# Cross attention and output stage in one program, the output weights split during the last groups, splits of the next batch's context on POOL

## The chip, the cores and the metric

One core of a Trainium2 chip runs the kernel. The metric is device time in microseconds of one execution; a row of runs is given by its median. The engines are TensorE (PE, and PEld for its weight loads), VectorE (DVE), ScalarE (ACT), GpSimd (POOL) and SyncE (SP), which issues all DMAs. Each engine works through its own instructions in order and waits on semaphores.

## The reference

A decoder block on x (4 batches of 256 rows, 512 wide) with a context of 1601 rows per batch, all in float32:

```python
x = _layernorm(x + _L0_attn_ref(x, w_qkv, w_o))                      # 32 heads of 128, 8 kv heads, causal, rotary
x = _layernorm(x + _L0_xattn_ref(x, ctx_4096, Wq, Wk, Wv, Wo))       # 16 heads of 96, 4 kv heads
x = _layernorm(x + _L0_ffn_ref(x, lora_A, lora_B, W, bias, lora_w))  # x @ W.T + bias + low-rank adapters
```

The cross attention takes its keys and values from the context and the latents together (1601 + 256 rows, padded to 1858):

```python
hidden = jnp.concatenate([context, latents], axis=1)
q, k, v = latents @ Wq.T, hidden @ Wk.T, hidden @ Wv.T
attn = softmax(q @ k / sqrt(96))
out = (attn @ v) @ Wo.T
```

## The kernel before

Three programs follow each other: `self_attention`, `cross_attention` and `finish`. Each has a block of its own, and a program begins only when all engines have ended the one before. All of TensorE's large products are taken with float32 operands split in two parts, a high part (a copy to the type float32r, made by ACT) and a low part (the difference from the original, made by DVE or POOL), and three products: high by high, high by low, low by high (`PARTS`).

`cross_attention` goes over the 4 batches. For each it projects keys and values from the context in seven chunks (`projection_steps`), whose splits are the steps "hidden": ACT copies the chunk of 128x1024 (L1004), POOL subtracts in four pieces of 128x256 (L1287). Then come 8 groups (4 kv heads by 2 halves of the queries) of 8 steps (`PAIRS`), 64 steps in a batch (`attention_steps`). A step k is for TensorE six matmuls of scores (L1132) and six of values for step k - 2 (L1145), and, except in the last group, two matmuls (L1103) for the row maxima of the next group. The eighth step of a group is half as long. ACT takes the exponential (L1202) into b_pf and copies its high part to b_pr (L989), DVE makes the low part (L995, both inputs in SBUF) and reduces the maxima (L1251). At j = 3 DVE works out the reciprocals of the row sums (L1263 to L1267), at j = 4 ACT spreads them (L1217) and POOL multiplies (L1294), whose result y SP stores to the tensor "attended". Queries are loaded into b_qraw per kv head and split in the steps "queries": ACT's copy L1174, POOL's subtraction L1298, both 96x1024, at j = 6 of groups 2 and 4. In groups 3 and 5 at j = 6 the first two context chunks of the next batch are split.

One schedule, `schedule_b`, lists the steps of all batches. Each engine runs through this list and does its own part of each step, in the list's order; what holds it is only the semaphores in its part. So an engine without a part in a step goes past it.

SP issues loads and stores in an order of its own (L1026 to L1062). In the last batch it loads for the output stage, as soon as the projections are done: the attended rows of batch 0 (`y_first`), the output weights (`wo_raw`), the feed weights (`wt`) and the adapters.

`finish` first splits the 12 pieces of the output weights and of batch 0's attended rows (ACT L1440 and L1437, DVE L1461, POOL L1510). Its TensorE part, for eight tiles of 128 rows, is `project(t)` (36 matmuls of 512 columns; ahead of the last nine stands `turn(t - 1)`, four transposes of the normed tile), then `feed(t - 1)` (12 matmuls with the feed weights). After the first tile stand the `adapters` (four float32 matmuls, whose results DVE adds to `wt`). DVE and ACT take the norms in the order of the list `norms`, each (t, 0) after the output product and (t, 1) after the feed; a norm is an add, statistics, a root on ACT (L1447), a reciprocal and a scaling (L1504). DVE makes the turned tile's low part (L1472) at the beginning of norm (t + 1, 0), for the last tile at the beginning of (7, 1). ACT copies its high part (L1455) behind the root of (t, 0).

## Time and profile before

| | us |
|---|---|
| median of 3 runs | 1933.54 (1930.08 to 1937.99) |
| the profiled execution | 1935.04 |
| its span, first to last instruction | 1933.2 |
| self attention and its hand-over | 0 to about 750 |
| four batches of cross attention | about 750 to 1815 |
| output stage | about 1817 to 1933 |

In rows of a timeline the columns are the start in us from the span's beginning, the duration in us, the engine, the line, the operation, output and inputs, the count, and in brackets the idle time before it with what ended it. A row can stand for several instructions in a run (xN), and its duration then reaches from the first to the last.

### The profile page before, as it was taken

Reading aid. Unit: us, or ns where it says so; the run is one execution under the profiler, and the core shown is the slowest. Engines: PE = TensorE matmul, PEld = TensorE weight load, DVE = VectorE, ACT = ScalarE, POOL = GpSimd, SP = SyncE. Lnnn points to the kernel's source line nnn. Section 1 sums busy time; section 2 is a strip of 40 time slices with the busy share of each in tenths; the row PEclk is TensorE's granted clock in tenths of the full one; section 3 lists DMA queues with packets and bytes.
Section 4 is the critical chain, followed back from the end, with each engine's and each line's share of the span. In section 5 each row is a group of like instructions: output and inputs, shape, how many; then the busy total and the mean of one; then the engine's idle time right before and its main releaser. Section 6 shows DMA issues by size and latency. Waiting matters only on the chain. (4 is left out here: it accounts for less than half of the span.)

```text
span 1933.2 us, 28030 instructions
## 1 busy us (share of the span) xinstructions
PE 1874.4 (97%) x9512; PEld 1542.0 (80%) x9512; DVE 1229.7 (64%) x2123; ACT 1184.8 (61%) x2081; POOL 654.3 (34%) x682
## 2 busy tenths in 40 slices
PE   7999999999999999999999999999999999999798
PEld 5888888888888788877779877788777798777576
DVE  4665656566566712577865678745778656787654
ACT  5666656666566633467775577764677755777620
POOL 5666757667576522101103011121011030110341
PEclk8999999999999999999999999999999999999899
DMA  4001101001010354100102000111001023000220
GB/s 170 28 28 28 48 11 49 27 27 43 11 54 13 114 193 126 55 5 17 28 20 79 11 9 27 28 39 55 5 17 28 20 77 133 9 17 9 90 82 27
DMA packets 59384, 89.84 MB, mean 46 GB/s; under 512 B 7060, under 2 KB 42260, under 8 KB 58518
## 3 DMA queue, kind: packets, MB, share of 16 engines
q1 hardware_dynamic: 59288, 88.57, 14.5%
...
## 5 line engine op out<-in xcount | busy, mean ns | idle before, releaser
L1145 PE MATMUL b_o_ps<-b_pr,b_v 128*97 128x512 f32 (+1 forms) x1440 | 376.2, 395 | 12.0 <-DVE b_pr L995 10.7
L1132 PE MATMUL b_s<-b_q,b_kt 97*128 97x512 f32 (+1 forms) x1440 | 374.8, 394 | 2.0 <-DVE b_v L1244 2.0
L1251 DVE TENSOR_REDUCE b_mx<-b_m 128x1 f32<-128x1024 f32 (+1 forms) x256 | 286.7, 1120 | 120.6 <-PE b_m L1103 119.3
L995 DVE TENSOR_TENSOR b_pr<-b_pf,b_pr 128x1024 fp32r<-128x1024 f32 (+1 forms) x256 | 310.1, 1211 | 67.6 <-ACT b_pr L989 67.6
L1202 ACT ACTIVATE b_pf<-b_s 128x1024 f32<-128x1024 f32 (+1 forms) x256 | 247.5, 967 | 135.8 <-PE b_s L1132 135.3
L1145 PEld LDWEIGHTS b_o_ps<-b_pr,b_v 128*97 128x97 f32 (+1 forms) x1440 | 231.8, 162 | 111.8 <-ACT b_pr L989 12.1
L1132 PEld LDWEIGHTS b_s<-b_q,b_kt 97*128 97x128 f32 (+1 forms) x1440 | 262.7, 185 | 64.6 <-issue 3.7
L1294 POOL TENSOR_TENSOR b_y<-b_recs,b_o 96x512 f32<-96x512 f32 x32 | 41.3, 1290 | 768.7 <-ACT b_recs L1217 768.7
L989 ACT ACTIVATE b_pr<-b_pf 128x1024 fp32r<-128x1024 f32 (+1 forms) x256 | 257.5, 1006 | 42.0 <-PE b_o_ps L1145 38.5
L445 PE MATMUL a_ring<-a_xt,w_a 128*128 128x512 f32 x1128 | 278.9, 398 | 0.0
L445 PEld LDWEIGHTS a_ring<-a_xt,w_a 128*128 128x128 f32 x1128 | 208.8, 191 | 41.0
L495 PE MATMUL a_ring<-a_wo,a_y 128*128 128x512 f32 x768 | 191.2, 398 | 0.0
L800 POOL TENSOR_TENSOR a_p<-a_p,a_rec 128x128 f32<-128x128 f32 (+1 forms) x256 | 130.5, 530 | 143.3 <-DVE a_rec L704 143.3
L495 PEld LDWEIGHTS a_ring<-a_wo,a_y 128*128 128x128 f32 x768 | 140.2, 189 | 29.2 <-DVE a_y L714 1.0
L1103 PE MATMUL b_m<-b_kt,b_q 96*128 96x512 f32 (+1 forms) x512 | 152.5, 379 | 1.8 <-DVE b_mx L1251 1.8
L1083 PE MATMUL b_s<-a_hid,w_kv 128*128 128x256 f32 (+1 forms) x1008 | 130.0, 286 | 6.8 <-issue 4.9
L1083 PEld LDWEIGHTS b_s<-a_hid,w_kv 128*128 128x128 f32 x1008 | 127.8, 189 | 9.4 <-issue 5.7
L605 ACT ACTIVATE a_p<-a_ms,a_top 128x128 f32<-128x128 f32 (+1 forms) x256 | 114.2, 448 | 31.0 <-DVE a_top L698 29.4
L1087 PE MATMUL b_s<-w_kv,a_hid 128*128 128x384 f32 (+1 forms) x720 | 133.0, 337 | 0.0
L698 DVE CUSTOM_DVE_ANT_0 a_ms<-a_s,a_mask 128x128 f32<-128x128 f32 (+1 forms) x256 | 81.1, 354 | 80.3 <-PE a_s L462 80.0
L1287 POOL TENSOR_TENSOR a_hid<-hraw,a_hid 128x256 fp32r<-128x256 f32 (+1 forms) x108 | 75.7, 732 | 165.0 <-ACT a_hid L1004 165.0
L1087 PEld LDWEIGHTS b_s<-w_kv,a_hid 128*128 128x128 f32 (+1 forms) x720 | 123.6, 184 | 3.3
...
## 6 DMA issues: line engine op xcount, KB each, us to landing
...
```

The lines of the kernel that those rows point to most:

```text
L445: mm = pe.matmul(bank[:], w[:, a, c, t * HD:(t + 1) * HD], xt[:, m, c, n * HALF:(n + 1) * HALF], start=i == 0, stop=i == 3 * C - 1)
L495: mm = pe.matmul(bank[:], y[:, b % 2, a, h, tt * P:(tt + 1) * P], wo[:, m, h, :], start=i == 0, stop=i == 3 * GRP - 1)
L800: pool.tensor_tensor(seen, seen, rec[:, h, qt:qt + 1].to_broadcast([P, (qt + 1) * P]), ALU.mult)\
L989: act.activation(pr[0:rows, k % 2, HI, 0:n], pf[0:rows, k % 2, 0:n], ACT.Copy).then_inc(p_hi.sem, 1)
L995: dve.tensor_tensor(pr[0:rows, k % 2, LO, 0:n], pf[0:rows, k % 2, 0:n], f(pr[0:rows, k % 2, HI, 0:n]), ALU.subtract).then_inc(p_lo.sem, 1)
L1083: mm = pe.matmul(bank[:, 0:n], w_k[:, a, c, i * P:(i + 1) * P], hid[:, j % 2, m, c, 0:n], start=s == 0, stop=s == 3 * C - 1)
L1087: mm = pe.matmul(bank[0:rows, 0:KV2 * HD2], hid[:, j % 2, a, c, t0 - c0:t0 - c0 + rows], w_v[:, m, c, :], start=s == 0, stop=s == 3 * C - 1)
L1103: mm = pe.matmul(ps_m[:, x:min(x + BANK, n)], q[0:HD2, kv % 2, HI, hp * BANK + t * P:hp * BANK + (t + 1) * P], kt[0:HD2, HI, kv, c0 + x:c0 ...
L1132: mm = pe.matmul(ps_s[k % 2][0:rows, i * BANK:(i + 1) * BANK], kt[:, a, kv, t0:t0 + rows], q[:, kv % 2, m, hp * BANK:(hp + 1) * BANK], sta ...
L1145: mm = pe.matmul(ps_o[0:HD2 + 1, :], v[0:rows, a, t, g // 2, :], pr[0:rows, k % 2, m, i * BANK:(i + 1) * BANK], start=t == 0 and s == 0, s ...
L1202: act.activation(pf[0:rows, k % 2, 0:n], ps_s[k % 2][0:rows, 0:n], ACT.Exp, scale=SCALE_B)\
L1251: dve.reduce_max(mx[:, g % 2, t, half:half + 1], ps_m[:, 0:MAXW[half][1]], X).then_inc(mx_made.sem, 1)
```

## The change

- `finish` is gone. Its tiles lie over SBUF and PSUM that the cross attention no longer needs in its last batch, so that it all is one block. For this b_v and b_kt are laid out by kv head first, and the kv heads' values stand in rotated order (`slot`, and the host's order of `wv`).
- In the last batch the 12 pieces of the output weights and batch 0's attended rows are split in steps "wo2", one in each step from group 6, j = 2 on: ACT copies the weights' piece (128x512); POOL copies and subtracts the rows' piece (128x256) and subtracts the weights' piece. DVE's scaling of the adapters' operand is a step at group 7, j = 2.
- The first tile of the output product (`output(0)`) stands ahead of the last two value steps and of the sums of the last group. The adapters follow, and their sums by DVE.
- The query splits for kv = 2 and 3 are done by POOL alone (a copy and a subtraction), listed at j = 1 instead of 6 of groups 2 and 4. The next batch's context splits in groups 3 and 5 are also done by POOL alone.
- The turned tile and the feed's PSUM have two buffers, x2 three. The order at the end changes: `output(7)` directly behind `output(6)`, then the feeds of tiles 5 and 6, the last transposes and the last feed; norm (5, 1) stands behind (7, 0).
- The loads of x1, of the bias and of batch 1's attended rows are issued earlier, in the last groups.

The core of the diff:

```diff
-def attention_steps():
+def attention_steps(last):
 
     s = []
+    work = [("wo2", k) for k in range(FT)]
...
-        if g in (2, 4) and j == 6:
-            s += [("queries", g // 2 + 1)]
+        if g in (2, 4) and j == 1:
+            s += [("queries", g // 2 + 1, "spare")]
         if g in (3, 5) and j == 6:
-            s += [("hidden", g // 2 - 1, "next")]
+            s += [("hidden", g // 2 - 1, "spare", "next")]
+        if last and work and (g == GROUPS - 2 and j >= 2 or g == GROUPS - 1):
+            s += [work.pop(0)]
+        if last and (g, j) == (GROUPS - 1, 2):
+            s += [("lora",)]
     return s + [("split", STEPS - 1)]
 
 
...
-    body = attention_steps()
     tail = [("pv", STEPS - 2), ("pv", STEPS - 1), ("sums", GROUPS - 1), ("spread", GROUPS - 1)]
     s = []
     for b in range(B):
         head = projection_steps(b > 0)
+        body = attention_steps(b + 1 == B)
         s += [(x, b) for x in (head if b == 0 else head[FRONT:])]
         if b + 1 == B:
-            s += [(x, b) for x in body + tail if x[-1] != "next"]
+            s += [(x, b) for x in body + [("first_rows",)] + tail if x[-1] != "next"]
             break
         s += [(x[:-1], b + 1) if x[-1] == "next" else (x, b) for x in body]
...
-        kt = sb("b_kt", [ROWB + 1, 2, KV2, S2], F32R)
-        v = sb("b_v", [P, 2, NT2, KV2, HD2 + 1], F32R)
+        v_mem = nc.sbuf_base
+        v = sb("b_v", [P, KV2, 2, NT2, HD2 + 1], F32R)
+        kt_mem = nc.sbuf_base
+        kt = sb("b_kt", [ROWB + 1, KV2, 2, S2], F32R)
+        q_mem = nc.sbuf_base
...
+        wo_s = over(early_mem, "c_wo", [P, 2, FT, D], F32R)
+        y0_mem = early_mem + 4 * 2 * FT * D
+        y_in0 = over(y0_mem, "c_y0", [P, 2, FT, T], F32R)
+        x2t_mem = y0_mem + 4 * 2 * FT * T
+        assert x2t_mem + 4 * 2 * D <= kt_mem + 3 * 4 * 2 * S2
+        x2t = [over(x2t_mem, "c_x2t0", [P, 2, D], F32R), over(v_mem, "c_x2t1", [P, 2, D], F32R)]
+        x2 = over(v_mem + 4 * 2 * D, "c_x2", [P, 3, D])
+        assert 4 * 5 * D <= v_head
+        y_in1 = over(w_mem, "c_y1", [P, 2, FT, T], F32R)
+        y_c = (y_in0, y_in1)
...
+        ps_w = [ps_s[0][:, i * BANK:(i + 1) * BANK] for i in range(2)]
+        ps_f = [ps_s[1][:, i * BANK:(i + 1) * BANK] for i in range(2)]
+        ps_y = [ps_m[:, i * BANK:(i + 1) * BANK] for i in range(2)]
...
+        norms = []
+        for t in range(TILES + 1):
+            norms += [(t, 0)] * (t < TILES) + [(t - 1, 1)] * (1 <= t < TILES - 1)
+        norms += [(TILES - 2, 1), (TILES - 1, 1)]
+        norms.remove((TILES - 3, 1))
+        norms.insert(norms.index((TILES - 1, 0)) + 1, (TILES - 3, 1))
+        nth = {x: i for i, x in enumerate(norms)}
...
+        def spare(arg):
+
+            return arg[-1] == "spare"
...
                 for g in range(GROUPS):
+                    if b == END and g == GROUPS - 1:
+
+                        sp.wait_ge(s_made.sem, s_made.at(b, STEPS))
+                        sp.dma_start(x1[:, 0:2, :], x1_dram[:, 0:2, :]).then_inc(x1_in[0], 16)
+                        load_attended(1)
+                        sp.dma_start(x1[:, 2:TILES, :], x1_dram[:, 2:TILES, :]).then_inc(x1_in[1], 16)
...
+                    if g == 4:
+                        sp.wait_ge(q_lo.sem, q_lo.at(b, KV2))
+                        if b + 1 < B:
+                            load_queries(b + 1, 0)
+                        else:
+                            sp.dma_start(bias_s[:], bias.to_broadcast([P, D])).then_inc(bias_in, 16)
...
+            for b in range(2, B):
+                sp.wait_ge(y_lo, FT * b)
+                load_attended(b)
...
+
+            def output(t):
+                b = t // 2
+                if t >= 2:
+                    pe.wait_ge(z_done, nth[(t - 2, 0)] + 1)
+                else:
+                    pe.wait_ge(mx_made.sem, mx_made.at(END, 8 * GROUPS))
+                for k in range(FT):
+                    if k == FT - 3 and t:
+                        turn(t - 1)
+                    if t % 2 == 0:
+                        pe.wait_ge(y_lo, FT * b + k + 1)
+                    if t == 0:
+                        pe.wait_ge(wo_lo, k + 1)
+                    for i, (a, m) in enumerate(PARTS):
+                        mm = pe.matmul(ps_y[t % 2], y_c[b % 2][:, a, k, (t % 2) * P:(t % 2 + 1) * P], wo_s[:, m, k, :],
+                                       start=k == 0 and i == 0, stop=k == FT - 1 and i == 2)
+                mm.then_inc(y_full, 1)
+
+            def turn(t):
+                pe.wait_ge(normed, nth[(t, 0)] + 1)
+                if t:
+                    pe.wait_ge(t_lo, t)
+                for c in range(C):
+                    mm = pe.transpose(ps_t[:, c * P:(c + 1) * P], x2[:, t % 3, c * P:(c + 1) * P], idf[:])
+                mm.then_inc(turned, 1)
+
+            def feed(t):
+                pe.wait_ge(t_hi, t + 1)
+                pe.wait_ge(t_lo, t + 1)
+                pe.wait_ge(w_lo, C)
+                if t >= 2:
+                    pe.wait_ge(z_done, nth[(t - 2, 1)] + 1)
+                i = 0
+                for c in range(C):
+                    for a, m in PARTS:
+                        mm = pe.matmul(ps_f[t % 2], x2t[t % 2][:, a, c * P:(c + 1) * P], ws[:, m, c, :], start=i == 0,
+                                       stop=i == 3 * C - 1)
+                        i += 1
+                mm.then_inc(f_full, 1)
+
+            def adapters():
+
+                pe.wait_ge(lb_done, 1)
+                pe.wait_ge(exp_done.sem, exp_done.at(END, STEPS))
+                for c in range(C):
+                    if c >= 2:
+                        pe.wait_ge(w_sum, c - 1)
+                    pe.matmul(ps_w[c % 2], la[:, c * P:(c + 1) * P], lb[:], start=True, stop=True).then_inc(w_full, 1)
 
...
+                elif kind == "first_rows":
+                    output(0)
 
             run(pe, handle)
+            adapters()
+            for t in range(1, TILES):
+                output(t)
+                if t < TILES - 2:
+                    feed(t - 1)
+            feed(TILES - 3)
+            feed(TILES - 2)
+            turn(TILES - 1)
+            feed(TILES - 1)
...
-                if kind == "hidden":
+                if kind == "hidden" and not spare(arg):
                     split_hidden(act, b, arg[0])
-                elif kind == "queries":
+                elif kind == "queries" and not spare(arg):
...
+                elif kind == "wo2":
+                    k = arg[0]
+                    if k == 0:
+                        act.wait_ge(late_in.sem, 16 * len(last_loads))
+
+                        act.wait_ge(pv_done.sem, pv_done.at(b, (GROUPS - 2) * PAIRS))
+                    act.activation(wo_s[:, HI, k, :], woraw[:, k, :], ACT.Copy).then_inc(wo_hi, 1)
...
+            act.wait_ge(pv_done.sem, pv_done.at(END, STEPS))
+            for c in range(C):
+                act.wait_ge(w_sum, c + 1)
+                act.activation(ws[:, HI, c, :], wt[:, c, :], ACT.Copy).then_inc(w_hi, 1)
+            for i, (t, which) in enumerate(norms):
+                act.wait_ge(eps_done, i + 1)
+                act.activation(std[:, i % 2:i % 2 + 1], mv[:, i % 2, 1:2], ACT.Sqrt).then_inc(std_done, 1)
+                if which == 0:
+                    if t % 2 == 0 and t // 2 + 1 < B:
+                        for k in range(0, FT, 4):
+                            split_y(t // 2 + 1, k, 4)
+                    act.wait_ge(turned, t + 1)
+                    if t >= 2:
+                        act.wait_ge(f_full, t - 1)
+                    act.activation(x2t[t % 2][:, HI, :], ps_t[:], ACT.Copy).then_inc(t_hi, 1)
...
+                elif kind == "lora":
+                    dve.wait_ge(late_in.sem, 16 * len(last_loads))
+                    dve.wait_ge(lw_in, 16)
+                    dve.tensor_scalar(lb, lb, lw[:, 0:1], ALPHA_OVER_RANK, ALU.mult, ALU.mult).then_inc(lb_done, 1)
...
+            dve.wait_ge(pv_done.sem, pv_done.at(END, STEPS))
             for c in range(C):
                 dve.wait_ge(w_full, c + 1)
-                dve.tensor_tensor(wt[:, c, :], ps_w[c % 2][:], wt[:, c, :], ALU.add).then_inc(w_sum, 1)
...
+                    if spare(arg):
+                        pool.wait_ge(h_in.sem, h_in.at(b, 16 * C * (j + 1)))
+
+                        pool.wait_ge(full.sem, full.at(b, 0))
+                        pool.tensor_copy(hid[:, j % 2, HI, :, 0:n], hraw[:, :, 0:n]).then_inc(h_hi.sem, 1)
...
+                elif kind == "wo2":
+                    k = arg[0]
+                    if k == 0:
+                        pool.wait_ge(late_in.sem, 16 * len(last_loads))
+                        pool.wait_ge(pv_done.sem, pv_done.at(b, (GROUPS - 2) * PAIRS))
+                    pool.tensor_copy(y_in0[:, HI, k, :], y_first[:, k, :]).then_inc(y_hi, 1)
+                    pool.wait_ge(y_hi, k + 1)
+                    pool.tensor_tensor(y_in0[:, LO, k, :], y_first[:, k, :], f(y_in0[:, HI, k, :]), ALU.subtract).then_inc(y_lo, 1)
+                    pool.wait_ge(wo_hi, k + 1)
+                    pool.tensor_tensor(wo_s[:, LO, k, :], woraw[:, k, :], f(wo_s[:, HI, k, :]), ALU.subtract).then_inc(wo_lo, 1)
...
+                    if spare(arg):
+                        pool.wait_ge(q_in.sem, q_in.at(b, 16 * (kv + 1)))
+
+                        pool.wait_ge(s_made.sem, s_made.at(b, (kv - 1) * 2 * PAIRS))
+                        pool.tensor_copy(q[0:HD2, kv % 2, HI, :], qraw[:]).then_inc(q_hi.sem, 1)
+                    pool.wait_ge(q_hi.sem, q_hi.at(b, kv + 1))
+                    pool.tensor_tensor(q[0:HD2, kv % 2, LO, :], qraw[:], f(q[0:HD2, kv % 2, HI, :]), ALU.subtract)\
```

## Rows read from the trace of the kernel before

**Rows 1.** The page: busy TensorE, clock granted in 40 slices, costliest group.
```profile
PE 1874.4 (97%) x9512; PEld 1542.0 (80%) x9512; DVE 1229.7 (64%) x2123; ACT 1184.8 (61%) x2081; POOL 654.3 (34%) x682
...
PEclk8999999999999999999999999999999999999899
...
L1145 PE MATMUL b_o_ps<-b_pr,b_v 128*97 128x512 f32 (+1 forms) x1440 | 376.2, 395 | 12.0 <-DVE b_pr L995 10.7
```

**Rows 2.** Timeline of POOL, y products of groups 3 and 4, later 2 to 4.
```profile
1171.49 1.28 POOL L1294 TENSOR_TENSOR b_y<-b_recs,b_o 96x512 f32<-96x512 f32 x1 [17.84 <-ACT b_recs L1217]
...
1196.34 1.29 POOL L1294 TENSOR_TENSOR b_y<-b_recs,b_o 96x512 f32<-96x512 f32 x1 [15.45 <-ACT b_recs L1217]
...
1678.88 1.28 POOL L1294 TENSOR_TENSOR b_y<-b_recs,b_o 96x512 f32<-96x512 f32 x1 [23.30 <-ACT b_recs L1217]
...
1704.74 1.30 POOL L1294 TENSOR_TENSOR b_y<-b_recs,b_o 96x512 f32<-96x512 f32 x1 [17.84 <-ACT b_recs L1217]
1729.19 1.29 POOL L1294 TENSOR_TENSOR b_y<-b_recs,b_o 96x512 f32<-96x512 f32 x1 [23.15 <-ACT b_recs L1217]
```

**Rows 3.** Timeline of the last batch, end of group 4, with a query split.
```profile
1733.66 1.04 ACT L1174 ACTIVATE b_q<-b_qraw 96x1024 fp32r<-96x1024 f32 x1
...
1734.79 2.40 POOL L1298 TENSOR_TENSOR b_q<-b_qraw,b_q 96x1024 fp32r<-96x1024 f32 x1 [4.30 <-ACT b_q L1174]
...
1735.69 2.58 DVE L995 TENSOR_TENSOR b_pr<-b_pf,b_pr 128x1024 fp32r<-128x1024 f32 x1
...
1738.42 1.59 PE L1145 MATMUL b_o_ps<-b_pr,b_v 128*97 128x512 f32 x6 [1.12 <-DVE b_pr L995]
```

**Rows 4.** Timeline of the last batch, end of group 5, without a split.
```profile
1760.13 0.85 PE L1132 MATMUL b_s<-b_q,b_kt 97*65 97x512 f32 x3
...
1761.47 1.22 DVE L995 TENSOR_TENSOR b_pr<-b_pf,b_pr 128x1024 fp32r<-128x1024 f32 x1
...
1762.95 1.57 PE L1145 MATMUL b_o_ps<-b_pr,b_v 128*97 128x512 f32 x6
```

**Rows 5.** Groups of POOL by form, whole span: busy us, mean ns, idle before.
```profile
L1287 POOL TENSOR_TENSOR a_hid<-hraw,a_hid 128x256 fp32r<-128x256 f32 x92 | 71.0, 803 | 136.5 <-ACT a_hid L1004 136.5
...
L1517 POOL TENSOR_TENSOR c_ws<-wt,c_ws 128x512 fp32r<-128x512 f32 x4 | 5.0, 1297 | 4.0 <-ACT c_ws L1444 4.0
```

**Rows 6.** Timeline of the hand-over from the attention to the output stage.
```profile
1807.38 1.56 PE L1145 MATMUL b_o_ps<-b_pr,b_v 128*97 128x512 f32 x6
...
1809.40 2.29 PE L1145 MATMUL b_o_ps<-b_pr,b_v 128*97 128x512 f32 x9 [0.46 <-DVE b_pr L995]
...
1813.37 0.70 DVE L1267 STREAM_TRANSPOSE b_recs<-b_rec 32x512 f32<-32x512 f32 x1
...
1817.51 0.63 ACT L1440 ACTIVATE c_wo<-wo_raw 128x512 fp32r<-128x512 f32 x1 [2.14 <-PEq L907]
...
1819.51 5.90 PE L1387 MATMUL c_y<-c_wo,c_y 128*128 128x512 f32 x15 [7.81 <-POOL c_y L1510]
...
1833.25 3.79 PE L1418 MATMUL c_w<-lora 128*128 128x512 f32 x8
...
1836.48 6.70 PE L1387 MATMUL c_y<-c_wo,c_y 128*128 128x512 f32 x27
```

**Rows 7.** Timeline of the tail, from the last tile's last nine output matmuls.
```profile
1914.07 2.31 PE L1387 MATMUL c_y<-c_wo,c_y 128*128 128x512 f32 x9
...
1916.52 3.06 PE L1408 MATMUL c_f_ps<-c_ws,c_x2t 128*128 128x512 f32 x12
...
1919.17 0.69 DVE L1488 TENSOR_TENSOR c_x<-c_x,c_bias 128x512 f32<-128x512 f32 x1
...
1919.41 0.60 PE L1396 MATMUL c_t_ps<-idf,c_x 128*128 128x128 f32 x4
...
1922.71 0.68 DVE L1472 TENSOR_TENSOR c_x2t<-c_t_ps,c_x2t 128x512 fp32r<-128x512 f32 x1
...
1923.49 4.38 PE L1408 MATMUL c_f_ps<-c_ws,c_x2t 128*128 128x512 f32 x12 [3.48 <-DVE c_x2t L1472]
```

289 lines of the change are left out of this document (91 added, 198 removed).

## The prediction

> **What bounds the kernel now.** I read the page's busy rows first, then its costliest groups with what ended their idle time, then the timeline where the diff touches. TensorE is busy for 97% of the span; the clock granted to it dips only at the start, at the change of stages and at the end [rows 1]. So a microsecond is won only where TensorE is idle or slowed by a feeder, and three such places lie in the diff: the waits for b_pr in the attention, 10.7 us in all [rows 1], the hand-over to the output stage (an idle time of 7.81, and a slow first tile) [rows 6], and the last feed (3.48) [rows 7]. The profiled run took 1935.04 us, 1.84 above its span; the median of the three runs is 1933.54, 1.5 less. I sum changes on the profiled span and take them from the median.
>
> **What the ACT splits cost in the attention.** The y products (L1294) stand once in each group, at j = 4, so their distance is a group's period. With a query split it is 1704.74 - 1678.88 = 25.86 us, without any split 24.45, with a context split 1196.34 - 1171.49 = 24.85 [rows 2]. The other groups repeat this within 0.15. So a query split costs some 1.3 us (two in each of four batches: 10.6) and a context split 0.35 (two in each of three batches: 2.1): 12.7 us at most.
>
> Why a query split costs that stands in one group end [rows 3]. ACT's copy of 1.04 us delays b_pr's high part. Then DVE's low part (L995) takes 2.58 us instead of 1.22 [rows 4]: POOL's L1298 runs from 1734.79 to 1737.19 and L995 ends 1.08 after that, so it waited for POOL's instruction and then ran. TensorE idles 1.12 us. This is a rule of the Trainium skill, page "SBUF — State Buffer", section "Who interferes with whom": a VectorE instruction with two SBUF inputs and a GpSimd instruction that reads SBUF exclude each other for a whole instruction. By that rule work moved to POOL is not free, and the trace agrees (2.58 against 1.22 us).
>
> **Query splits on POOL.** The step stands at j = 1, but POOL knows only its own order: behind the y product of the group before, it waits for q_in and for the last scores of the old keys. So it starts right behind the last scores of the group before. For kv = 2 the load has landed long before. At such a group end [rows 4] the last scores end at 1760.98, L995 starts at 1761.47 and ends at 1762.69, and the matmul that needs it starts at 1762.95: a slack of about 0.1 us beside 0.15 of signalling. POOL's copy would start 0.1 behind the scores, 0.4 ahead of L995. With a copy of C us, L995 ends at 1761.1 + C + 1.08, and TensorE waits C - 0.65. No row shows a POOL copy. The nearest is the subtraction of the same 96x1024 tile from two inputs, 2.40 us [rows 3], my upper bound; half of it, 1.2, is the lower one, as a copy reads half as much. I take 1.5, nearer to the half because the second input is the main difference. Wait 0.85 instead of 1.3: 0.45 won four times, 1.8 us (bounds -1.8 and +3.0). The Trainium skill, page "GPSIMD Engine Reference", section "Performance versus the Vector engine", has 769 ns for a tight loop over 512 elements of one input, which would be an estimate of 1.54 us for 1024; no row can show it. The subtraction behind the copy meets only the low part of the short last step, whose matmul stands behind twelve matmuls of scores; nothing is lost there.
> For kv = 3 the load is issued behind the y product of j = 4 and lands 4 to 6 us later, when L995 has begun; in three batches POOL also has the context split ahead of it. L995 then mostly goes first. I take 1.0 of 1.3 won, four times: 4.0 us (bounds 1.5 and 5.2).
> **Context splits on POOL.** POOL starts them, too, right behind the y product. ACT's share of the 0.35 goes. But the four subtractions, 0.80 us each in the mean [rows 5], then reach over the group end with its slack of 0.1, and each can hold L995. I take 0.1 won six times: 0.6 us (bounds -1.5 and +2.1). The transfers that wait for these parts are issued a group later, so none comes late.
> Sum in the attention: 1.8 + 4.0 + 0.6 = 6.4 us won (bounds -1.8 and +10.3).
>
> **Output weights split in groups 6 and 7.** Before, the twelve pieces were split in the open: the first output matmul is at 1819.51, the adapters only at 1833.25 [rows 6]. Now ACT has one copy more per step, 0.63 us [rows 6], where it idles 0.4 to 0.7 us ahead of its high parts and exponentials, so the high part comes about 0.1 later, and up to 0.7 right behind the spread copies. POOL has per step a copy of 128x256 (0.3 to 0.6), a subtraction of that size (0.7) and one of 128x512 (1.30) [rows 5]: 2.3 to 2.6. With the 1.08 of L995, which excludes them [rows 3], that is 3.4 to 3.7 us for a step of 24.45 / 8 = 3.06 [rows 2]. L995 waits for the rest of POOL's current instruction, 0.45 in the mean and 1.3 at worst, with a slack of 0.5 to 1.4 inside a group. I take 1.5 us lost (bounds 0 and 5); DVE's one scaling of the adapters' operand, new in group 7, is in that bound.
> POOL itself comes late, but for whom? It can start behind pv(47), at about 1768.5. Twelve pieces of 2.5 and two y products of 1.3 are 32.6 us. Until 1807.5, the last scores, there are 39, less 15 low parts of 1.08, plus 2 in which waits of both overlap: 25. So the last piece is ready at 1807.5 + 7.6 = 1815.1. TensorE reaches it behind pv(61) and eleven pieces: 1807.4 + 1.4 + 11 x 0.69 = 1816.4. I take 0.5 us lost (bounds 0 and 4). Group 6's y product stands behind ten pieces on POOL, at about 1809. For it wait the copy of o of group 7 (due at 1819) and, on SP, its store and the loads of x1 and of the next attended rows behind that.
>
> **The hand-over.** Before: from pv(61) at 1807.38 to the second tile at 1836.48, 29.1 us [rows 6]. After, in TensorE's order and at 1.39 us for six matmuls of 512 columns (half of the 2.78 that a feed adds): pv(61) 1.39, the 36 matmuls of the first tile 8.33, the 9 of pv(62) and pv(63) 2.08, sum 11.8. Then four adapters of (1836.48 - 1833.25) / 4 = 0.81 each. Two run at once; the third waits for DVE's first sum, now behind the sums of group 7. These reached before from 1811.69 to 1814.07 [rows 6], 2.4 us; with 0.7 for the sum and 0.15 of signalling it is 3.3, of which two adapters cover 1.6. So 5.0 us instead of 3.2, in all 16.8: 12.3 less (bounds 11 and 13). The half-speed matmuls behind the idle 7.81 are in the 29.1 already. The first norm and its table load are hidden by 27 matmuls (6.3 us) ahead of the first transposes, against about 5 us of DVE and ACT. The loads of x1 and of the next attended rows, issued near 1810 now, land in 4 to 13 us; the first rows of x1 are due at 1825, the attended rows at 1828.
>
> **The tail.** The pace of a tile stays, since the low part of the turned tile sets each feed as before. At the end feed(5) goes behind output(7), and DVE has norm (7,0), then (5,1), (6,1), and only then the last turned tile's low part. Before, feed(7) starts 7.1 us after the end of output(7) at 1916.38 [rows 7]. After, counted from that end: (7,0) is done at 2.9. (5,1) needs a root from ACT, but ACT first waits for the last transposes, which stand behind two feeds (2 x 2.89, 0.1, 0.6: 6.5), and copies for 0.6, so (5,1) ends near 8.0. (6,1) takes 3.5 (1919.17 to 1922.71), the low part 0.7 [rows 7]: feed(7) starts at 12.3. Output(7) ends 2.9 earlier, since feed(5) is not ahead of it. 12.3 - 2.9 - 7.1 = 2.3 us later. TensorE idles 5.7 us ahead of it instead of 3.48, and its 12 matmuls took 4.38 there against 3.06 before the pause [rows 7]: 0 to 0.8 more, I take 0.4. Tail: 2.7 us lost (bounds 2 and 3.5).
>
> **Sum.** 1933.54 - 12.3 - 6.4 + 1.5 + 0.5 + 2.7 = 1919.5, given as 1920 us. The new layouts of kt and v alter neither instructions nor sizes. This case alone lies within 1914 to 1925.
>
> **Rivals.**
> *POOL's copy is as slow as its subtraction.* C = 2.4: the kv = 2 splits lose 1.8 instead of winning 1.8, the context splits lose 1, each piece costs POOL 0.3 more and the first tile waits 4 us. 3.6 + 1.6 + 3.5 = 8.7 more: 1928 us. The change would then not do what it says, as POOL has no spare time that counts. For it: all of POOL's rows have nearly one rate per element [rows 3, 5]. Against: all have two inputs.
> *All of the splits' cost is won.* 12.7 instead of 6.4, and the pieces cost nothing: 1912 us. For it: POOL's long idle times [rows 2]. Against: the slack of 0.1 [rows 4].
> *The new order hides the tail.* If the last low part waited for no norm, feed(7) would start at 8.0 - 2.9, 2.0 earlier than before: 1920 - 4.7 = 1915 us. Against: DVE's program order.
> *POOL's pieces starve L995: slower than before.* If POOL is never idle in the last two groups, every L995 may meet a fresh 1.30 us subtraction, and a low part held like that cost 1.1 us [rows 3]. 14 steps x 1.1 = 15.4, and 4 us of backlog in the first tile: 19.4 in place of 2.0 gives 1937 us, and beyond 1943 if the copies are slow as well. It decides from the point where POOL's instructions and L995 exceed a step's 3.06 us, which they do by 0.3 to 0.6. Against it: L995 meets the start of the long one only now and then.
>
> **Chances.** Forecast 0.50, slow copy 0.20, all won 0.15, tail hidden 0.10, L995 starved 0.05. The range reaches over the slow copy and the full gain: 1911 to 1929. A measurement can tell about 0.5%, 9.7 us, from no change, so faster means below 1923.9. Faster: 0.43 of the forecast, 0.15, 0.10: 0.68. Same: 0.07 + 0.20 + 0.02 = 0.29. Slower 0.03.
>
> **What would show it.** The first output matmul right behind pv(61); 5 us for the adapters with a wait of 1.7; POOL's copy ahead of an L995 of 2 us and more at the end of group 1; L995 at 1.2 to 2.5 in groups 6 and 7; group periods of 24.5 to 25.4 in place of 25.86; an idle time of 5 to 6 us ahead of the last feed. I am wrong if no L995 waits for the copy, if the first tile waits for pieces for over 4 us, or if the last feed follows output(7) in less than 11 us.

## The result and the profile after

| | before | after |
|---|---|---|
| median, us | 1935.73 (11 runs, 1930.08 to 1937.99) | 1925.87 (11 runs, 1923.79 to 1931.16) |
| the profiled execution, its span | 1935.04, 1933.2 | 1924.93, 1923.0 |
| ratio after / before | | 0.9956, interval 0.9946 to 0.9966 |

The change wins 0.4%: 8.5 us of 1935 by the ratio (6.6 to 10.5), 10.2 by the two profiled spans. Expected were 14. (The median of before is here that of 11 runs, 2.2 us above the median of three that the prediction subtracts from.) The page of after, its busy rows, the granted clock in 40 slices and the first group of TensorE:

```profile
PE 1870.8 (97%) x9512; PEld 1541.8 (80%) x9512; DVE 1231.2 (64%) x2111; ACT 1168.6 (61%) x2055; POOL 708.7 (37%) x720
...
PEclk8999999999999999999999999999999999999999
...
L1234 PE MATMUL b_o_ps<-b_pr,b_v 128*97 128x512 f32 (+1 forms) x1440 | 375.9, 394 | 5.5 <-DVE b_pr L1061 4.9
```

The waits for b_pr fell from 10.7 us [rows 1] to 4.9, and in this row the granted clock no longer dips at the change of stages. In finer windows it still does, only later: it is 1.00 from 1800 to 1822 us, then 0.76 from 1822 to 1828.2, where TensorE stands idle, and 0.56 from 1828.2 to 1832.5. L1234, L1061 and L1253 of after are L1145, L995 and L1387 of before.

**Attention.** (pv(k) stands for the value matmuls of step k, output(t) for the output product of tile t, counted from 0.) The timeline of after at the end of a group with a query split for kv = 2 (POOL, DVE, TensorE), then y products of POOL:

```profile
859.34 1.03 POOL L1539 CAST b_q<-b_qraw 96x1024 fp32r<-96x1024 f32 x1 [4.80 <-PE b_s L1221]
859.69 1.76 DVE L1061 TENSOR_TENSOR b_pr<-b_pf,b_pr 128x1024 fp32r<-128x1024 f32 x1
860.46 3.26 POOL L1541 TENSOR_TENSOR b_q<-b_qraw,b_q 96x1024 fp32r<-96x1024 f32 x1
861.60 1.61 PE L1234 MATMUL b_o_ps<-b_pr,b_v 128*97 128x512 f32 x6 [0.25 <-DVE b_pr L1061]
...
853.25 1.29 POOL L1532 TENSOR_TENSOR b_y<-b_recs,b_o 96x512 f32<-96x512 f32 x1 [59.88 <-ACT b_recs L1370]
...
878.23 1.29 POOL L1532 TENSOR_TENSOR b_y<-b_recs,b_o 96x512 f32<-96x512 f32 x1 [14.51 <-ACT b_recs L1370]
902.78 1.29 POOL L1532 TENSOR_TENSOR b_y<-b_recs,b_o 96x512 f32<-96x512 f32 x1 [23.27 <-ACT b_recs L1370]
...
927.76 1.29 POOL L1532 TENSOR_TENSOR b_y<-b_recs,b_o 96x512 f32<-96x512 f32 x1 [13.38 <-ACT b_recs L1370]
```

POOL's copy takes 1.03 us, not 1.5. DVE's low part starts 0.35 behind the copy's start, waits for its end and then runs (1.76 in place of 1.22 [rows 4]); POOL's subtraction, next in line, is held by it in turn (3.26 for 2.40). The first period (853.25 to 878.23) has the kv = 2 copy in it and is 24.98. The second, which held a query split before and took 25.86 [rows 2], is 24.55. The third has the context split and behind it the kv = 3 split, and is 24.98; with the context split alone it took 24.85 before [rows 2]. The periods of the other batches repeat these within 0.03; in the last one, without a context split, the third is 25.09. So 0.4 is still lost to each kv = 2 copy and to each context split, and 0.5 to the kv = 3 split of the last batch, where no context split stands ahead of it.

**Groups 6 and 7 and the hand-over.** The longest of two waits for b_pr in groups 6 and 7, then TensorE over the hand-over (last scores' values, first tile, adapters three and four, second tile):

```profile
1783.00 1.30 POOL L1526 TENSOR_TENSOR c_wo<-wo_raw,c_wo 128x512 fp32r<-128x512 f32 x1
1783.47 1.92 DVE L1061 TENSOR_TENSOR b_pr<-b_pf,b_pr 128x1024 fp32r<-128x1024 f32 x1 [3.44 <-ACT b_pr L1055]
1785.49 1.60 PE L1234 MATMUL b_o_ps<-b_pr,b_v 128*97 128x512 f32 x6 [1.10 <-DVE b_pr L1061]
...
1799.03 1.60 PE L1234 MATMUL b_o_ps<-b_pr,b_v 128*97 128x512 f32 x6
...
1800.47 8.34 PE L1253 MATMUL b_m<-c_wo,c_y 128*128 128x512 f32 x36
...
1813.90 1.98 PE L1286 MATMUL b_s<-lora 128*128 128x512 f32 x4 [1.29 <-DVE wt L1456]
...
1815.32 6.71 PE L1253 MATMUL b_m<-c_wo,c_y 128*128 128x512 f32 x27
```

The first tile runs its 36 matmuls without a pause in 8.34 us, and from pv(61) to the second tile it is 16.3 us; before it was 29.1 [rows 6].

**The new pause.** Between the second tile and the first turned tile (timeline of POOL, DVE and TensorE):

```profile
1815.88 5.05 POOL L1548 TENSOR_TENSOR c_ws<-wt,c_ws 128x512 fp32r<-128x512 f32 x4
...
1818.83 0.17 DVE L1491 RECIPROCAL c_rstd<-c_std 128x1 f32<-128x1 f32 x1 [0.48 <-ACT c_std L1389]
1819.03 9.17 DVE L1493 TENSOR_SCALAR c_x<-c_x,c_mv,c_rstd 128x512 f32<-128x512 f32 x1
1820.90 7.01 POOL L1552 TENSOR_TENSOR c_y<-c_yraw,c_y 128x1024 fp32r<-128x1024 f32 x3
1828.25 1.12 PE L1262 MATMUL b_x<-idf,c_x 128*128 128x128 f32 x4 [6.23 <-DVE c_x L1493]
```

The norm is ready to scale at 1819.03, well ahead of the transposes' due time of 1822.0 (1815.32 + 6.71). But the scaling, 0.55 us elsewhere, takes 9.17. POOL makes the low parts of the feed weights (four) and of batch 1's attended rows (three) in one row without a gap, and the scaling ends at 1828.20, 0.29 behind POOL's last. TensorE idles 6.23 us; the transposes (1.12 for 0.60) and the nine matmuls behind them (3.69 for 2.33) run slowly for a while: the granted clock is 0.56 there, so mostly at its lower level, 1.2 GHz, and 1.00 from 1832.5 on. From the start of output(1) to that of output(2) it was 11.85 us before and is 19.99 after: 8.1 us.

**The tail.** DVE from the scaling of norm (6,1), then the last feed and the last scaling:

```profile
1911.12 0.55 DVE L1493 TENSOR_SCALAR c_z<-c_z,c_mv,c_rstd 128x512 f32<-128x512 f32 x1
1911.59 0.68 DVE L1461 TENSOR_TENSOR c_x2t<-b_x,c_x2t 128x512 fp32r<-128x512 f32 x1
...
1912.37 5.28 PE L1274 MATMUL b_s<-c_ws,c_x2t 128*128 128x512 f32 x12 [5.74 <-issue]
...
1919.98 0.55 DVE L1493 TENSOR_SCALAR c_z<-c_z,c_mv,c_rstd 128x512 f32<-128x512 f32 x1
```

TensorE's idle time of 5.74 us ends with the last low part (L1461), made from 1911.59 to 1912.27. Output(7) ends near 1900.5; the last feed starts 11.9 later, behind the low part that stands behind norms (5,1) and (6,1), and takes 5.28 us in place of 4.38 [rows 7].

The difference of the spans, piece by piece: start of the attention -1.9 (the self attention's code is the same; this start lay anywhere from 742 to 747 in the kernels run here), attention -7.7, pieces in groups 6 and 7 +1.4 (27.79 to 29.23 from the y product made in group 6 to pv(61)), hand-over -12.8, the new pause +8.1, start of the last feed +1.9, its slower matmuls +0.9. The sum is -10.1 of -10.2.

### The profile page after: what moved, and what is told of

It reads as the page before. It is cut to its first block, busy times and chain, and to the rows that moved or that the text cites. A ratio compares the mean times of both kernels' runs of the same rounds, so it can differ in the third digit from the quotient of the medians.

```text
span 1923.0 us, 28030 instructions
## 1 busy us (share of the span) xinstructions
PE 1870.8 (97%) x9512; PEld 1541.8 (80%) x9512; DVE 1231.2 (64%) x2111; ACT 1168.6 (61%) x2055; POOL 708.7 (37%) x720
## 4 chain that ended last, share of the span: by engine, by line
PE 55%; DVE 4%; issue 1%; ACT 1%; POOLq 0%; ACTq 0%
PE b_o_ps L1234 16%; PE b_s L1221 16%; PE b_s L1172 7%; PE b_s L1176 6%; PE b_m L1192 5%; PE b_m L1253 3%; DVE b_pr L1061 1%; PE b_s L1274 1%; DVE b_mx L1428 1%; DVE c_x L1493 0%; PE b_x L1262 0%; ACT b_pf L1348 0%; DVE b_kt L1417 0%; ACT b_pr L1055 0%; PE b_x L1203 0%
## 5 line engine op out<-in xcount | busy, mean ns | idle before, releaser
L1234 PE MATMUL b_o_ps<-b_pr,b_v 128*97 128x512 f32 (+1 forms) x1440 | 375.9, 394 | 5.5 <-DVE b_pr L1061 4.9
L1061 DVE TENSOR_TENSOR b_pr<-b_pf,b_pr 128x1024 fp32r<-128x1024 f32 (+1 forms) x256 | 317.1, 1239 | 66.5 <-ACT b_pr L1055 66.5
L1234 PEld LDWEIGHTS b_o_ps<-b_pr,b_v 128*97 128x97 f32 (+1 forms) x1440 | 231.8, 162 | 104.7 <-issue 13.2
L772 POOL TENSOR_TENSOR a_swapped<-a_swapped,a_sin 128x512 f32<-128x512 f32 x80 | 106.5, 1332 | 54.5 <-ACT a_swapped L585 54.5
```

The source lines that it names most:

```text
L1061: dve.tensor_tensor(pr[0:rows, k % 2, LO, 0:n], pf[0:rows, k % 2, 0:n], f(pr[0:rows, k % 2, HI, 0:n]), ALU.subtract).then_inc(p_lo.sem, 1)
L1234: mm = pe.matmul(ps_o[0:HD2 + 1, :], v[0:rows, slot(g // 2), a, t, :], pr[0:rows, k % 2, m, i * BANK:(i + 1) * BANK], start=t == 0 and s = ...
```

## The experiments

All are edits of the changed kernel; lines are those of their own text. Where only one run was made, the trace is the result, and its time stands beside it. The theory (A where the expectations use letters): the missing gain is this one scaling, held by POOL's row of subtractions.

**POOL holds back (e1_pool_holds).**

```diff
+                if b == 1:
+                    pool.wait_ge(normed, 1)
                 for k in range(0, FT, 4):
```

> The changed kernel, but POOL waits for the first norm (normed of tile 0) before it subtracts batch 1's attended rows. Theory A (POOL's back-to-back instructions starve DVE's scaling L1493, which took 9.17 us): L1493 of tile 0 ends within 2.5 us of its start (behind what is left of the four feed-weight subtractions), TensorE's wait of 6.2 us ahead of the first transposes is gone, and with the clock kept the run is 7 to 8 us shorter than the changed kernel, near 1918. Rival B (the norm is late for another reason, as x1 arriving late or ACT's table load): the wait stays at about 6 us and the time stays near 1926.

Measured: 1918.56 us (1918.41 to 1921.19), ratio to before 0.992 (0.9903 to 0.9936), so 7.3 below the changed kernel by medians. From the second tile's start to the end it is 99.5 us by the traces, in place of 107.7, so 8.2 less; but its groups 6 and 7 took 2.2 us more than those of after, for a reason that no edit touches (see the half pieces below). Its timeline at the same place:

```profile
1817.80 5.06 POOL L1548 TENSOR_TENSOR c_ws<-wt,c_ws 128x512 fp32r<-128x512 f32 x4
1820.95 2.19 DVE L1493 TENSOR_SCALAR c_x<-c_x,c_mv,c_rstd 128x512 f32<-128x512 f32 x1
1823.28 7.19 POOL L1554 TENSOR_TENSOR c_y<-c_yraw,c_y 128x1024 fp32r<-128x1024 f32 x3 [0.42 <-DVE c_x L1493]
```

With nothing behind the four feed-weight parts the scaling ends 0.28 behind them and TensorE doesn't wait. That the pause is caused by POOL, and its price, are shown. Even here the scaling, at hand from 1820.95, was passed over at the boundary of POOL's third and fourth instruction, near 1821.6.

**Small pieces (e2_small_pieces).** Batch 1's three subtractions in twelve of 128x256.

```diff
-                    pool.tensor_tensor(y_c[b % 2][:, LO, k:k + 4, :], y_later[:, k:k + 4, :],
-                                       f(y_c[b % 2][:, HI, k:k + 4, :]), ALU.subtract).then_inc(y_lo, 4)
+                    n = 1 if b == 1 else 4
+                    for i in range(k, k + 4, n):
+                        pool.tensor_tensor(y_c[b % 2][:, LO, i:i + n, :], y_later[:, i:i + n, :],
+                                           f(y_c[b % 2][:, HI, i:i + n, :]), ALU.subtract).then_inc(y_lo, n)
```

> The changed kernel, but batch 1's attended rows are subtracted in twelve pieces of 128x256 instead of three of 128x1024, back to back. Theory A1 (DVE's two-port scaling gets no turn as long as POOL's next instruction is there): L1493 still takes 8 to 10 us. Theory A2 (it waits for the one instruction in progress, as L1061 does): L1493 takes under 2 us, and TensorE's wait ahead of the first transposes is gone.

Measured: 1926.10 us in one run.

```profile
1818.35 10.40 DVE L1493 TENSOR_SCALAR c_x<-c_x,c_mv,c_rstd 128x512 f32<-128x512 f32 x1
1820.22 8.24 POOL L1554 TENSOR_TENSOR c_y<-c_yraw,c_y 128x256 fp32r<-128x256 f32 x12
```

From 1818.35 on POOL passes thirteen boundaries, those between the pieces 0.7 us apart, and the scaling gets none of them. So it isn't the length of POOL's instructions. What is left is that the next one follows without a gap, which e11 tests.

**Another form of the scaling (e3_one_port, e9_two_inputs).** In e3 the first scaling is one of 511 columns and one of a single column; in e9 it is two instructions with two inputs each in SBUF, beside the small pieces.

```diff
+                if (t, which) == (0, 0):
+                    dve.tensor_scalar(row[:, 0:D - 1], row[:, 0:D - 1], mv[:, s, 0:1], rstd[:, s:s + 1], ALU.subtract, ALU.mult)
+                    row = row[:, D - 1:D]
```

```diff
+                if (t, which) == (0, 0):
+                    dve.tensor_tensor(row, row, mv[:, s, 0:1].to_broadcast([P, D]), ALU.subtract).then_inc(shifted, 1)
+                    dve.wait_ge(shifted, 1)
+                    dve.tensor_tensor(row, row, rstd[:, s:s + 1].to_broadcast([P, D]), ALU.mult).then_inc(normed, 1)
+                    continue
```

> The changed kernel, but the scaling of tile 0's norm is cut into 511 columns and 1 column, so that its width is odd and its rate per column should fall from the 0.55 us per 512 seen in the quiet tail to about 0.65. If the long wait belongs to the double-rate form of this one-input instruction, the two together take under 1.2 us beside POOL's subtractions and TensorE's wait is gone (7 to 8 us shorter). If any DVE instruction is held by POOL's row of subtractions, it stays at 6 us.

> As e2_small_pieces (POOL's twelve pieces of 128x256 back to back), but the scaling of tile 0's norm is done by two instructions with two SBUF inputs each (the row and the mean or the root spread over it), like the low parts that waited for one POOL instruction only. If such instructions get a turn between two of POOL's, each waits 1.3 us at most, both together take under 4 us, and TensorE's wait ahead of the first transposes (7.5 us in e2_small_pieces) is gone. If POOL's row of instructions starves every DVE instruction that shares its port, they end only behind it, some 10 us later.

Measured: 1923.77 and 1925.72 us, one run each. DVE's first instruction in e3, then in e9:

```profile
1818.12 9.17 DVE L1494 TENSOR_SCALAR c_x<-c_x,c_mv,c_rstd 128x511 f32<-128x511 f32 x1
```

```profile
1816.27 10.66 DVE L1495 TENSOR_TENSOR c_x<-c_x,c_mv 128x512 f32<-128x512 f32 x1
```

e3 decides nothing: an odd width was to give the scaling another form, but 511 columns still end 0.28 us behind POOL, as 512 did, so the run doesn't show that it did. e9 shows that an instruction with two inputs is passed over as well, so the form of the scaling isn't the cause.

**A gap between POOL's instructions (e11_drain).** Same work, same order; POOL waits for its own instruction before it issues the next.

```diff
+                if c:
+                    pool.wait_ge(w_lo, c)
                 pool.tensor_tensor(ws[:, LO, c, :], wt[:, c, :], f(ws[:, HI, c, :]), ALU.subtract).then_inc(w_lo, 1)
...
+                    if b == 1:
+                        pool.wait_ge(w_lo, C)
+                        pool.wait_ge(y_lo, FT * b + k)
```

> The changed kernel in which POOL, in its row of seven subtractions behind the adapters, waits for its own instruction before it issues the next (the four of the feed weights and the three of batch 1's attended rows). The work and its order are the same; only a short pause comes between two instructions. If DVE's first scaling (9.17 us in the changed kernel) goes without its turn because POOL's next instruction is already issued when the running one ends, the pause lets it in at the next end: 0.6 to 3.5 us, the idle time ahead of the first turned tile shrinks from 6.2 to under 1.5, and the one run is about 1919. If a pause of that size doesn't matter (POOL stays ahead of DVE at each new start), the scaling still ends just behind POOL's last subtraction, 8 to 11 us long, with a time of 1925 to 1929.

Measured: 1918.13 us in one run.

```profile
1817.70 5.61 POOL L1550 TENSOR_TENSOR c_ws<-wt,c_ws 128x512 fp32r<-128x512 f32 x4
...
1820.85 1.30 DVE L1493 TENSOR_SCALAR c_x<-c_x,c_mv,c_rstd 128x512 f32<-128x512 f32 x1
```

The four take 5.61 instead of 5.05 us, so their starts lie 0.19 further apart. (One of them lasts 1.29, so 0.15 us lies between the end of one record and the start of the next; without the wait the records meet.) The scaling now ends at 1822.15, behind POOL's third instruction, and no idle time stands ahead of the transposes. From the second tile's start to the end it is 99.1 us in place of 107.7: the whole 8.1 and some 0.5 of slow matmuls in the tail. So this small gap was enough for a scaling that was already waiting. The next scaling, at 1828.71 (2.77 us), still lost one turn: it began in a gap, but had to wait for a POOL instruction whose start is recorded 0.05 behind its own.

**The old order of the tail, and the low part earlier (e4_old_tail, e5_early_split).** e4 puts the feeds and norms back in the order of before; e5 in addition makes the last turned tile's low part ahead of norm (6,1).

```diff
-            norms += [(t, 0)] * (t < TILES) + [(t - 1, 1)] * (1 <= t < TILES - 1)
-        norms += [(TILES - 2, 1), (TILES - 1, 1)]
-        norms.remove((TILES - 3, 1))
-        norms.insert(norms.index((TILES - 1, 0)) + 1, (TILES - 3, 1))
+            norms += [(t, 0)] * (t < TILES) + [(t - 1, 1)] * (t >= 1)
...
-                if t < TILES - 2:
-                    feed(t - 1)
-            feed(TILES - 3)
-            feed(TILES - 2)
+                feed(t - 1)
```

```diff
-                    if t == TILES - 1:
-                        split_turned(t)
+                    if t == TILES - 2:
+                        split_turned(t + 1)
```

> The changed kernel with the order of feeds and norms at the end as before the change (feed(t-1) behind each output(t), norm (5,1) ahead of (7,0)). By the prediction's account of the tail: output(7) ends 2.9 us later, the last feed starts 7.1 us after it instead of 11.9 and takes 4.4 us instead of 5.3, so the run is 2.8 to 3.3 us shorter than the changed kernel. Rival (the new order hides the tail): it is 2 us longer.

> The order at the end as before the change (as in e4_old_tail), and DVE's low part of the last turned tile ahead of norm (6,1) instead of behind it. If the last feed hangs on DVE's order alone, it starts about 5.1 us after output(7)'s end (7.15 in e4_old_tail, 11.9 in the changed kernel) and, with a shorter pause, takes 3.5 to 4.4 us: 2 to 3 us shorter than e4_old_tail, 4 to 5 us shorter than the changed kernel, near 1921. If the norms set the end (DVE's chain (6,1), (7,1) runs on either way), the last feed is early but the end moves by under 1 us against e4_old_tail.

Measured: e4 1925.44 us (1924.26 to 1928.65), ratio 0.9957 (0.9943 to 0.9972); e5 1922.80 (1919.78 to 1926.97), ratio 0.9945 (0.9928 to 0.9961). The last feed of e4, then of e5 with the last scaling:

```profile
1913.31 4.57 PE L1271 MATMUL b_s<-c_ws,c_x2t 128*128 128x512 f32 x12 [3.53 <-issue]
```

```profile
1914.29 3.04 PE L1271 MATMUL b_s<-c_ws,c_x2t 128*128 128x512 f32 x12 [1.46 <-ACT c_x2t L1391]
...
1920.70 0.55 DVE L1487 TENSOR_SCALAR c_z<-c_z,c_mv,c_rstd 128x512 f32<-128x512 f32 x1
```

In e4 output(6)'s start lies 37.9 us before the end, in the changed kernel 40.1: the new order costs 2.2 us by the traces. The medians differ by only 0.4 and the spans by 0.2 the other way. The traces show why: from the y product made in group 6 to the second tile e4 took 47.7 us and after 45.5, and these 2.2 undo the 2.2 of the tail. So the cost of the order is shown by the traces alone. In e5 the last feed starts 5.05 us behind output(7) and runs at its full pace, 3.04. The end is then set by DVE: the norms (6,1) and (7,1) follow each other without a pause, and the last scaling ends 12.0 us behind output(7). The rival by which the last low part would wait for no norm was thus real as a mechanism, but it isn't what the change does.

**ACT splits again (e6_act_splits).** The query and context splits go back to ACT, the query splits also to j = 6 (ACT again waits for the last scores of the old keys).

```diff
-        if g in (2, 4) and j == 1:
-            s += [("queries", g // 2 + 1, "spare")]
+        if g in (2, 4) and j == 6:
+            s += [("queries", g // 2 + 1)]
         if g in (3, 5) and j == 6:
-            s += [("hidden", g // 2 - 1, "spare", "next")]
+            s += [("hidden", g // 2 - 1, "next")]
```

> The changed kernel with only one part undone: ACT makes the high parts of the queries (at j = 6) and of the next batch's context again. By the periods of the two traces (2.04 us won in each of the first three batches, 1.62 in the last) it is 7.7 us longer than the changed kernel, near 1933.6, with group periods of 25.8 at the query splits and L1061 (the low part) at 2.6 us there. The prediction's term was 6.4 us. If the gain of the attention is a matter of the run and not of the splits, the difference is under 3 us.

Measured: 1936.90 us (1931.91 to 1938.92), ratio 1.0012 (1.0002 to 1.0023). Two y products, a query split between them:

```profile
1193.85 1.30 POOL L1534 TENSOR_TENSOR b_y<-b_recs,b_o 96x512 f32<-96x512 f32 x1 [15.46 <-ACT b_recs L1372]
1219.69 1.30 POOL L1534 TENSOR_TENSOR b_y<-b_recs,b_o 96x512 f32<-96x512 f32 x1 [17.83 <-ACT b_recs L1372]
```

The period is 25.84 again. The profiled span is 7.1 above the changed kernel's, near the 7.7 expected from the periods; the medians say 11, and what the rest is stays open. So without the splits on POOL the change wins nothing: its hand-over gain of 12.8 is given back in the new pause (8.1), the tail (2.8) and the waits in groups 6 and 7 (1.5 in this run).

**The copy behind the low part (e7_copy_later).**

```diff
                         pool.wait_ge(s_made.sem, s_made.at(b, (kv - 1) * 2 * PAIRS))
+                        pool.wait_ge(p_lo.sem, p_lo.at(b, (kv - 1) * 2 * PAIRS - 1))
                         pool.tensor_copy(q[0:HD2, kv % 2, HI, :], qraw[:]).then_inc(q_hi.sem, 1)
```

> The changed kernel, but POOL waits, ahead of its query copy, for the low part of step 6 of the group that is ending. If the 0.4 us that a group with the kv = 2 split still costs (24.97 against 24.56) is the low part waiting behind POOL's 1.03 us copy, the period falls to 24.6 or less and no low part there takes over 1.4 us. The subtraction (2.4 us) then reaches over the short last low part, which has time for it. If the subtraction costs it, the period stays or grows.

Measured: 1927.57 us in one run (against after its attention began 2.3 us later, its groups 6 and 7 took 2.2 more, and 36 matmuls of a projection took 1.5 more; see the half pieces and the end of this text). POOL's copy and DVE's low part, at the group end shown above for after:

```profile
861.92 1.22 DVE L1061 TENSOR_TENSOR b_pr<-b_pf,b_pr 128x1024 fp32r<-128x1024 f32 x1
863.29 1.03 POOL L1540 CAST b_q<-b_qraw 96x1024 fp32r<-96x1024 f32 x1 [6.52 <-DVE b_pr L1061]
```

The low part runs its 1.22 again and the kv = 2 period falls from 24.98 to 24.51 in all four batches; so does the kv = 3 period of the last batch, from 25.09 to 24.55. The context periods stay at 24.98. The copy ahead of the low part was the 0.4, and 2.4 us in all.

**Half pieces in groups 6 and 7 (e10_half_pieces).**

```diff
-                    pool.tensor_tensor(wo_s[:, LO, k, :], woraw[:, k, :], f(wo_s[:, HI, k, :]), ALU.subtract).then_inc(wo_lo, 1)
+                    for i in range(0, D, D // 2):
+                        s = pool.tensor_tensor(wo_s[:, LO, k, i:i + D // 2], woraw[:, k, i:i + D // 2],
+                                               f(wo_s[:, HI, k, i:i + D // 2]), ALU.subtract)
+                    s.then_inc(wo_lo, 1)
```

> The changed kernel with POOL's subtraction of each output weight piece in two halves of 128x256 instead of one of 128x512, in groups 6 and 7. If TensorE's waits there come from a low part of DVE that has to wait for the rest of POOL's running instruction, as I hold, no wait for b_pr in these groups is longer than 0.7 us (half of the long instruction's 1.3 and a little), and their sum is 0.3 to 1.0 where the changed kernel has 1.5 and most of its variants 3.3. If instead DVE needs POOL to pause, or POOL's total work counts (now slightly more, 12 extra starts of some 0.06), the sum is 1.5 to 3.5 or more and single waits still reach 1.1 to 1.5. The time moves by at most 3 us, less than one look can tell; the waits are the result.

Measured: 1926.24 us in one run. TensorE's waits for b_pr in the two groups are 0.49, 0.65 and 0.37:

```profile
1785.61 1.61 PE L1234 MATMUL b_o_ps<-b_pr,b_v 128*97 128x512 f32 x6 [0.65 <-DVE b_pr L1061]
...
1800.96 7.66 PE L1253 MATMUL b_m<-c_wo,c_y 128*128 128x512 f32 x33
...
1809.24 0.94 PE L1253 MATMUL b_m<-c_wo,c_y 128*128 128x512 f32 x3 [0.62 <-POOL c_wo L1527]
```

The longest wait is 0.65, so a low part does wait for one running POOL instruction here. But the sum, 1.51, is that of the changed kernel (0.42 + 1.10), against 3.3 in e1, e2, e3, e4, e5, e7 and e8 (e8: 1.54, 0.94, 0.40 and 0.43), whose edits don't touch these groups in the last batch. With the larger sum it is 47.7 us from the y product made in group 6 to the second tile, with the smaller one (after, e6, e9, e11) 45.5, in e10 46.3. What decides between the two patterns isn't shown. A single run can differ from another by these 2.2 us, whatever its edit does elsewhere. And POOL, with twelve more starts, now comes late: its last piece ends at 1809.09 and the first tile stands 0.62 us for it. So I was wrong to expect 0.3 to 1.0.

**All together (e8_all, e12_all_half).** e8 has the edits of e1, e5 and e7 at once, e12 those and the half pieces.

> Four edits together on the changed kernel: POOL waits for the first norm before batch 1's attended rows (as in the first experiment), the old order of the tail with the last turned tile's low part ahead of norm (6,1) (as in the fifth), and POOL's copy of the kv = 2 queries behind the low part (as in the seventh). If the three gains lie at different places and simply add, as I hold: -7.3 (hold, by medians of the first experiment) -3.1 (tail, by medians of the fifth) and -1.6 (four copies of 0.4) from 1925.9, which gives 1913.9; 1911 to 1917 is within what self attention's own start varies. The idle time ahead of the first turned tile is gone and DVE's first scaling takes under 2.5 us; the last feed starts about 5 us after the end of output(7). If a pause that is filled only moves the end to the next limit (the attended rows of batch 1, or DVE's norms), less than two thirds of it comes: 1918 or more, with a new wait ahead of output(2) or at the end.

> The edits of the combined kernel and in addition the half pieces of POOL's output weights. If both work as I hold, it is 0.5 to 3 us below the combined kernel: 1911 to 1914, with no wait for b_pr in groups 6 and 7 above 0.7. If the halves do nothing for the waits, the two are within 1 us of each other.

Measured: e8 1912.81 us (1910.29 to 1913.02), ratio 0.9882 (0.9865 to 0.9899); e12 1911.72 (1909.26 to 1914.07), ratio 0.9885 (0.9868 to 0.9902). The two can't be told apart by medians; from the y product made in group 6 to the second tile e12 takes 46.3 us and e8 47.7, so by the traces the half pieces save 1.4 against this pattern. Both beat both kernels: by 22 to 23 us the one before, by 13 to 14 the changed one, where 12 had been expected of e8. The first turned tile and the last feed in e8:

```profile
1820.12 2.19 DVE L1487 TENSOR_SCALAR c_x<-c_x,c_mv,c_rstd 128x512 f32<-128x512 f32 x1
...
1822.95 0.60 PE L1259 MATMUL b_x<-idf,c_x 128*128 128x128 f32 x4
...
1901.66 3.04 PE L1271 MATMUL b_s<-c_ws,c_x2t 128*128 128x512 f32 x12 [1.46 <-ACT c_x2t L1391]
```

The first pause is gone, and ahead of the last feed 1.46 us are left of 5.74. From the second tile to the end it is 94.7 us (107.7 in the changed kernel, 96.7 before). The gains add, as they lie at different places of TensorE's chain.

## Why the prediction came out as it did

The sign, the size's order and the places were right; the forecast of 1920 us lay 6 below the measured median. Of these, 2.2 are the median of before, which is 1935.73 with 11 runs and was 1933.54 with three. The measured 1925.87 is 0.9 above the range given for this case alone (1914 to 1925). It lies in the full range only by the room left for the slow copy, which didn't come; that part of the hit is luck. "Faster", below 1923.9, had a chance of 0.68 and didn't come; the 0.29 for "same" did, though the interval shows a gain. None of the signs listed looked at the place where the time was lost. By its own steps, with the spans:

- **Hand-over, 12.3 forecast, 12.8 measured.** Right. The adapters take 4.6 us (1810.73 to 1815.32) with a wait of 1.29, for 5.0 and 1.7.
- **"The first norm and its table load are hidden by 27 matmuls."** This is the step that failed, at a cost of 8.1 us. The other terms came out at 16.3 us won, for 14.0; with the pause 8.2 is left, and the measured ratio says 8.5 (the spans have 1.9 more by the earlier start of the attention, which isn't the change's). So errors of the other terms hid 2.3 us of this one. The count of DVE's and ACT's time was good: the scaling was at hand 3.0 us before the transposes were due. I priced it at its busy time and never asked what POOL does meanwhile. Before, a gap of 0.27 us stood between the feed weights' parts and the attended rows' parts on POOL, and the same scaling, begun at 1840.19, took 0.88 (rows below). POOL's row then began 4.45 us ahead of the scaling and ended just before ACT's first copy of the attended rows. Now the last y product (1814.64 to 1815.91) stands right ahead of the row, which begins 3.15 us ahead of the scaling; the copy is ready when the fourth part ends, and no gap is left. e1 and e11 show it, each by taking away a different part of the cause: what follows the running instruction, and the lack of a gap.
```profile
1835.74 5.04 POOL L1517 TENSOR_TENSOR c_ws<-wt,c_ws 128x512 fp32r<-128x512 f32 x4 [3.96 <-ACT c_ws L1444]
...
1840.19 0.88 DVE L1504 TENSOR_SCALAR c_x<-c_x,c_mv,c_rstd 128x512 f32<-128x512 f32 x1
1841.05 7.12 POOL L1510 TENSOR_TENSOR c_y<-c_yraw,c_y 128x1024 fp32r<-128x1024 f32 x3 [0.27 <-ACT c_y L1437]
```

- **Attention, 6.4 forecast, 7.7 measured.** The mechanism was right: a wait of C - 0.65 with C = 1.03 is 0.38; the period was 0.4 longer than before and 0.5 longer than in e7, which took it away. The undersized terms are the copy (1.5 taken, 1.03 measured) and the kv = 3 splits (1.0 of 1.3 taken; in three batches all of it was won). The rate that the Trainium skill gives for a tight loop of one input (page "GPSIMD Engine Reference", section "Performance versus the Vector engine") led to an estimate of 1.54; the trace has 1.03, and decides. The context splits won nothing where I had 0.6: their period is 24.98, 0.1 above that of before.
- **Pieces in groups 6 and 7, 1.5 lost forecast, 1.4 measured**, though 3.3 in most other kernels with the same groups. L1061 was held for 0 to 0.7 us in after, up to 1.1 in e8. The rival in which these pieces starve the low part didn't come: here DVE got its turn at the first boundary each time.
- **First tile waits for the last piece, 0.5 forecast, none measured.** The whole attention ends 8.4 us earlier, so these times must be counted from pv(61) (1799.03 now). The last piece was ready 8.5 us behind it, at 1807.54, for 7.7 worked out; so POOL's work was counted 0.8 too low, not too high. TensorE came to that piece about 0.4 us later. It didn't wait, but by a small margin, as e10 shows with its 0.62.
- **Tail, 2.3 and 0.4 forecast, 1.9 and 0.9 measured.** The last feed 11.9 behind output(7), for 12.3; the idle time 5.74, for 5.7. The matmuls behind it were slowed more (5.28 us for 12) than I took, though 4.71 in e11.
- **A row misread.** The prediction has the clock dip "at the end [rows 1]"; the slices there show 9. A finer window does show it, 0.67 from 1923.4 to 1928 in before. No term of the sum rests on this.
- **Rivals.** The slow copy is refuted by 1.03 us. Of the splits' whole cost of 12.7 us 7.7 was won, so that rival failed too. The tail wasn't hidden.

**What stays open.** In the attention a low part of DVE that meets a row of POOL instructions got its turn at the first boundary: L1061 at 1783.47 above, and L995 in the kernel before, which took 1.62 us amid four subtractions of 128x256:

```profile
1177.08 3.81 POOL L1287 TENSOR_TENSOR a_hid<-hraw,a_hid 128x256 fp32r<-128x256 f32 x4 [4.31 <-ACT a_hid L1004]
1177.98 1.62 DVE L995 TENSOR_TENSOR b_pr<-b_pf,b_pr 128x1024 fp32r<-128x1024 f32 x1
```

In the first norm DVE's instruction got none of four boundaries (after) or thirteen (e2 and e9). Neither the length of POOL's instructions (e2), nor the number of inputs of DVE's (e9) explains the difference (neither 1024 columns nor an fp32r output was tried on DVE's side there); a scaling of DVE in group 7 (the adapters' operand, at 1787.48, 1.53 us) waited for one instruction only. Shown is that without a gap it can be passed over until POOL's row ends, and that gaps of 0.15 us ended that in e11. The Trainium skill, page "SBUF — State Buffer", section "Who interferes with whom", says: "Whoever issues first gets the shared pair for the whole instruction". The trace agrees at the group end shown first: the low part waits for the copy that began 0.35 ahead of it, and POOL's subtraction then waits for the low part. The second scaling of e11 doesn't fit, if the records' starts are taken as the order: recorded 0.05 ahead of POOL's instruction, it waited for it to end. Who is next when an instruction ends the sentence doesn't say, and by the traces here that need not be the one that has waited.
